# Cross-attention's sums turned through DRAM instead of by TensorE, one hop every half turn, in a fused decoder layer

## The reference, cut to what matters

```python
x = layernorm(x + self_attention(x))          # 16 heads of 16, causal over 64 rows
x = layernorm(x + cross_attention(x, c))      # channels = the 64 rows, time = the 256 columns
x = layernorm(x + feed_forward(x))            # 256 -> 1024 -> 256, quantised activations and weights

# cross_attention, b = 32, 8 heads of 8 channels, 256 positions each
q = rotary(split_heads(Wq @ x + bq)); k = rotary(split_heads(Wk @ c + bk)); v = split_heads(Wv @ c + bv)
p = softmax(einsum('bhtc,bhsc->bhts', q, k) / sqrt(8))
out = einsum('bhts,bhsc->bhtc', p, v)         # 256 x 8 per head
y = Wo @ out.transpose(0, 1, 3, 2).reshape(b, 64, 256) + bo
```

## Time and profile before

| | |
|---|---|
| median of 3 runs | 563.03 us (562.54 to 566.03) |
| the profiled execution | 563.8 us, of which its span is 561.9 us |
| PE busy | 450.6 us, 80% of the span |
| DVE busy | 442.4 us, 79% |
| ACT busy | 382.0 us, 68% |
| POOL busy | 289.6 us, 52% |
| granted TensorE clock, mean | 0.848 |
| DMA | 37.07 MB; the SP queue's packets took 22.8% of 16 engines' span |

### The profile page before, as it was taken

How to read it: one execution, slowest core, us unless ns; L and a number is a source line. 1 busy time by engine, 2 the same in 40 slices (tenths; PEclk the granted TensorE clock), 3 DMA queues, 4 the chain that set the end, 5 groups by cost and what they waited for, 6 DMA issues and landing times. The chain is left out here.

```text
span 561.9 us, 12026 instructions
## 1 busy us (share of the span) xinstructions
PE 450.6 (80%) x4162; PEld 243.0 (43%) x4162; DVE 442.4 (79%) x965; ACT 382.0 (68%) x698; POOL 289.6 (52%) x387
## 2 busy tenths in 40 slices
PE   6568799999999999999999999889877701555563
PEld 5354545555545555555555555433333200333342
DVE  2656687888988979889889798865848959999973
ACT  2222266767767667676676686687767787999972
POOL 5742565447555574475555744620032727667652
PEclk9677799999999999999999999975987875555555
DMA  6134318233242242332422323210000000000010
GB/s 217 48 97 149 97 46 248 66 92 91 57 111 67 64 110 60 90 91 60 108 69 64 106 61 82 71 56 1 3 1 1 1 0 1 10 28 19 30 37 29
DMA packets 51674, 37.07 MB, mean 66 GB/s; under 512 B 21408, under 2 KB 47648, under 8 KB 51488
## 3 DMA queue, kind: packets, MB, share of 16 engines
q1 hardware_dynamic: 51328, 36.10, 22.8%
q10 hardware_dynamic: 288, 0.23, 0.2%
HBM read 24.52 MB, written 10.49 MB: 62 GB/s over the span
## 5 line engine op out<-in xcount | busy, mean ns | idle before, releaser
L970 DVE TENSOR_REDUCE MX<-mx_b 128x2 f32<-128x512 f32 x256 | 167.8, 679 | 37.6 <-PE mx_b L581 36.4
L775 ACT ACTIVATE PB<-e_b 128x512 f32<-128x512 f32 x256 | 149.6, 592 | 64.7 <-PE e_b L609 63.8
L581 PE MATMUL mx_b<-KA,QA 48*128 48x256 bf16 x512 | 100.8, 282 | 10.3 <-DVE MX L970 10.1
L609 PE MATMUL e_b<-QA,KA 50*128 50x256 bf16 x512 | 100.9, 281 | 2.7 <-ACT PB L775 2.1
L626 PE MATMUL u_b<-PB,VA 128*32 128x256 f32 x1024 | 86.2, 404 | 3.4 <-ACT PB L775 2.9
L897 POOL TENSOR_TENSOR SP<-SP,srec 128x1024 f32<-128x1024 f32 x15 | 28.5, 1901 | 79.0 <-DVE srec L942 79.0
L581 PEld LDWEIGHTS mx_b<-KA,QA 48*128 48x128 bf16 x512 | 30.1, 95 | 88.5 <-issue 48.9
L1238 POOL TENSOR_TENSOR H<-H,row_tab 128x1024 f32<-128x1024 f32 x16 | 37.8, 2359 | 22.9 <-ACT H L1196 19.5
L1285 PE MATMUL r_b<-identh,Q 128*128 128x128 f16 x128 | 16.6, 311 | 39.5 <-ACT Q L1206 39.5
L1291 PE MATMUL z_b<-w2q,Q2T 128*128 128x256 bf16 x128 | 30.2, 417 | 19.3 <-ACT Q2T L1217 19.3
L314 POOL TENSOR_TENSOR rs<-mv,epsc 128x1 f32<-128x1 f32 x32 | 6.1, 189 | 72.5 <-DVE mv L301 50.2
(11 more groups left out here) (169 smaller groups left out, 1048.4 us busy)
## 6 DMA issues: line engine op xcount, KB each, us to landing
KA<-parts_k SPq DMA_DIRECT2D x64, 96.0 KB
QA<-parts_q SPq DMA_DIRECT2D x64, 96.0 KB
parts_q<-part_q SPq DMA_DIRECT2D x32, 128.0 KB, 2.0
parts_k<-part_k SPq DMA_DIRECT2D x16, 192.0 KB, 2.1
C<-in_ctx SPq DMA_DIRECT2D x16, 128.0 KB, 3.0
X<-in_x SPq DMA_DIRECT2D x16, 128.0 KB, 2.9
out_y<-O SPq DMA_DIRECT2D x16, 128.0 KB, 1.7
XT<-in_xT SPq DMA_DIRECT2D x15, 128.0 KB, 2.2
```

What stands on the lines that cost most here:

```text
L581: m = nc.tensor.matmul(mx_b[n % 2][:, D * k:D * k + D], QA[low:low + K_MAX, 2 * i.ring + b, h, P * u:P * u + P], KA[low:low + K_MAX, 2 * i ...
L609: m = nc.tensor.matmul(e_b[n % 2][:, D * k:D * k + D], KA[low:low + K_EXP, 2 * i.ring + b, h, P * sc:P * sc + P], QA[low:low + K_EXP, 2 * ...
L775: nc.scalar.activation(PB[:, n % 4].rearrange("p e t -> p (e t)"), e_b[n % 2][:, :], ACT.Exp, scale=XC ** -0.5).then_inc(e_sb.sem, 1)
L970: nc.vector.tensor_reduce(MX[:, b, e, 2 * q:2 * q + 2, u], mx_b[n % 2][:, :].rearrange("p (e s) -> p e s", e=2), AXL.X, ALU.max).then_inc( ...
```

## The change

The transposes that turn the sums, and the copy and the multiplications between them, are taken out. Instead:

- ACT writes `US` to a DRAM buffer (`store_sums`, two transfers of 256 KB per pair, at step 1 and step 9), right after its own copies.
- SP reads it back turned (`load_sums`): the denominators as `S32` (128 x 32, 16 KB) and the sums as `UV` (128 x 256, 128 KB), in the middle of the next turn.
- DVE takes one reciprocal of 128 x 32 (`reciprocals`, step 13). SP writes these 16 KB out (`recip_out`) and reads them back repeated over the channels (`recip_in`, 128 KB, into `RB`).
- POOL multiplies `UV` by `RB` into `AT` (`means`), one turn later than the means were made before. `x_out_proj` and all that follows for a pair are thus one turn later (`late` = pair `i-2` instead of `prev`).
- In the last turn two pairs pass through these steps: pair 13 (`late`) and pair 14 (`prev`), and the factors of pairs 0 to 13 are made at its end. Pair 15 passes through them in the second block, at later turns than before.
- The values' bias is folded into the output's once, in turn 0 (`value_bias`). The channel order of Wo is permuted on the host.
- In SP's turn the fan-out of the keys moves from the end of a turn to a place behind `max_rows(i, 1)` of the next, ahead of `load_c`.
- The identity table for the mask's product is written by two copies instead of one addition.

```diff
-        RD = sb("RD", [P, 16])
-        AN = sb("AN", [P, 2, 2, SEQ])
+        UV, RB = sb("UV", [P, D]), sb("RB", [P, D])
+        S32 = sb("S32", [P, 32])
...
+        def store_sums(sp, i, b):
+            if has(i, 2):
+                sp.wait_ge(ld_uv, 16 * (i.v - 1))
+                sp.wait_ge(ld_us, 16 * (i.v - 1))
+            wait(sp, u_sb, i, b + 1)
+            sp.dma_start(u_hbm[i.p][:, :, b].rearrange("c j x -> j c x"), US[:].rearrange("p s t -> p (s t)")).then_inc(moved[b], 16)
+
+        def load_sums(sp, i):
+            if has(i, 1):
+                wait(sp, at_sb, i.plus(-1), 1)
+            for b in range(2):
+                sp.wait_ge(moved[b], 16 * (i.v + 1))
+            flat = u_hbm[i.p].rearrange("c j b x -> c (j b x)")
+            sp.dma_start(S32[:], flat[XC:XC + 1].rearrange("c (r t) -> (c r) t", t=32)).then_inc(ld_us, 16)
+            sp.dma_start(UV[:], flat[0:XC].rearrange("c (r t) -> (c r) t", t=D)).then_inc(ld_uv, 16)
+
+        def recip_out(sp, i):
+            wait(sp, u_rec, i, 1)
...
+            sp.dma_start(rec_hbm.rearrange("h (k t) -> (h k) t", t=32), S32[:]).then_inc(rec_out, 16)
+
+        def recip_in(sp, i):
+            sp.wait_ge(rec_out, 16 * (i.v + 1))
+            sp.dma_start(RB[:], rec_hbm.unsqueeze(0).broadcast_to([XC, 16, D])).then_inc(rec_in, 16)
+
+        def reciprocals(dve, i):
+            dve.wait_ge(ld_us, 16 * (i.v + 1))
+            nc.vector.reciprocal(S32[:], S32[:]).then_inc(u_rec.sem, 1)
+
+        def means(pool, i):
+            pool.wait_ge(ld_uv, 16 * (i.v + 1))
+            pool.wait_ge(rec_in, 16 * (i.v + 1))
...
+            nc.gpsimd.tensor_tensor(AT[:], UV[:], RB[:], ALU.mult).then_inc(at_sb.sem, 1)
...
 # SP, body(i)
-                if i.v >= 1 and real(a):
-                    load_c(a)
                 if real(i):
                     max_rows(i, 1)
+                if i.v == NPAIR - 1:
+                    load_sums(sp, prev)
+                    recip_out(sp, prev)
+                    recip_in(sp, prev)
+                if i.v >= 0 and real(j):
+                    expand_rows("k", j)
+                if i.v >= 1 and real(a):
+                    load_c(a)
...
-                if real(a):
-                    expand_rows("k", a)
...
 # PE, body(i)
-                    if s == 3 and real(prev):
-                        u_transpose(pe, prev, 1, use(g_b[2], u_nrm, prev, 4))
-                    if s == 5 and real(prev):
-                        att_transpose(pe, prev, use(g_b[2], at_sb, prev, 1))
-                    if s == 9 and real(prev):
-                        x_out_proj(pe, prev, use(g_b[1], ln2, prev, 1))
+                    if s == 9 and real(late):
+                        x_out_proj(pe, late, use(g_b[1], ln2, late, 1))
+                    if s == 12 and i.v == NPAIR - 1:
+                        x_out_proj(pe, prev, use(g_b[2], ln2, prev, 1))
-                    if s == 13 and real(i):
-                        u_transpose(pe, i, 0, use(g_b[1], u_nrm, i, 2))
...
 # DVE, body(i)
-                    if s == 4 and i.v == NPAIR - 1:
+                    if s == 13 and i.v == NPAIR - 1:
                         mean_square(dve, 0)
-                    if s == 11 and i.v == NPAIR - 1:
-                        factors(dve, 0)
+                    if s == 15 and i.v == NPAIR - 1:
+                        factors(dve, 0)
+                        norm2_max(dve, prev)
...
 # POOL, body(i)
                 if i.v == NPAIR - 1:
+                    means(pool, late)
+                if real(late):
+                    rstd(pool, ln2, late, mv2, rs2)
+                if i.v == NPAIR - 1:
+                    means(pool, prev)
                     mean_power(pool, 0)
-                if real(prev):
                     rstd(pool, ln2, prev, mv2, rs2)
...
 # second block: pair 15, turns of the first product
+            load_sums(sp, last)
+            recip_out(sp, last)
+            recip_in(sp, last)
...
-                if t == 3:
+                if t == 6:
                     x_out_proj(pe, last, g_b[1])
...
-                if t == 1:
-                    u_norm(dve, last, 1, 1)
+                if t == 2:
+                    reciprocals(dve, last)
```

More of the change, by code:

```diff
@@ L238, in tile_at @@
             return i.plus(n // 16), n % 16
[L241 to L255, removed]
         def x_out_proj(pe, i, ps):
@@ L259, in x_out_proj @@
             nc.tensor.matmul(ps[:, 0:D], xw["o"], AT[:, :], start=True, stop=True).then_inc(xo_ps.sem, 1)
[L261 to L266, removed]
         def square_sum(act, i):
@@ new lines, in recip_in @@
+        def recip_in(sp, i):
[7 more added lines that the diff above has]
+            pool.wait_ge(rec_in, 16 * (i.v + 1))
+            if has(i, 1):
+                wait(pool, xo_ps, i.plus(-1), 1)
+            nc.gpsimd.tensor_tensor(AT[:], UV[:], RB[:], ALU.mult).then_inc(at_sb.sem, 1)
@@ L449, in body @@
                     store_parts("q", j)
+                if real(prev) and real(nxt):
+                    load_sums(sp, prev)
                 if real(nxt):
@@ L629, in pv_quad, with value_bias @@
                 last.then_inc(pv.sem, 1)
+            def value_bias(g):
+                ps = use(g_b[g], Event(s_bias, 0), Pair(0, 0), 1)
+                pe.wait_ge(ld_cross, NCROSS)
+                nc.tensor.matmul(ps[:, 0:1], xw["o"], xb["v"], start=True, stop=True).then_inc(s_bias_ps, 1)
             def weight_total(g):
@@ L859, in body @@
                         u_copy(i, 0)
+                    if s == 9 and real(i):
+                        store_sums(act, i, 0)
                     if s == 9 and real(nxt):
@@ L863, in body @@
                         pt_copy(a)
-                    if s == 13 and real(prev):
-                        norm2(act, prev)
+                    if s == (13 if real(nxt) else 12) and real(late):
+                        norm2(act, late)
+                    if s == (15 if real(nxt) else 12) and real(late):
+                        square_sum(act, late)
                     if s == 13 and real(a):
@@ L879, in _ @@
             u_copy(Pair(0, NPAIR - 1), 1)
+            store_sums(act, Pair(0, NPAIR - 1), 1)
         def k_mask(eng, ops, a, c, ev):
@@ L1116, in body @@
                     split_parts(pool, nc.gpsimd, "q", j)
+                if real(late) and real(nxt):
+                    means(pool, late)
                 if real(a):
@@ L1251, in _ @@
             mean_power(pool, 1)
+            means(pool, last)
             rstd(pool, ln2, last, mv2, rs2)
-            mean_power(pool, 2)
             for n in range(NPAIR):
+                if n == 5:
+                    mean_power(pool, 2)
                 wait(pool, qb, Pair(0, n), 1)
```

111 lines of the change are left out of this document (58 added, 53 removed).

## The result

The changed kernel takes **578.9 us** (median of 4 runs, 575.1 to 582.7) beside 564.5 for the kernel before on the same chip: ratio 1.025, 95% interval 1.017 to 1.034. Forecast were 556.8 and a range of 550 to 566. The profiled execution took 577.14, with a span of 575.0 against 561.9 and a granted clock of 0.819 against 0.848. Ratios, here and in the experiments, leave out executions more than 1.5% above the fastest of the same kernel.

A forecast was written before the change was run, and what follows sets the result against it. PE and DVE were taken to bound a turn by stretches, PE from step 13 to the next step 4. Terms -9.4 - 2.0 + 6.1 - 1.0 = -6.3 us against the profiled 563.8 gave 556.8 against the median, range 550 to 566.

The forecast's parts named there:

- Step 13: First block's turn: four transposes leave PE, one reciprocal replaces DVE's reciprocal and product; 0.57 us saved per turn.
- step 3: First block's turn: transposes go, but ACT's store issue of 0.43 us delays `MR`; 0.15 us saved, ends nothing and 0.59.
- lower end of 0.15 per turn: Smallest saving given for a steady turn of the first block, -2.0 us over 13 turns.
- first rival: Steady turns: both groups of transposes paid in full, 1.15 us per turn, total 551 us; chance 0.20.
- The Trainium skill's 50 ns: ACT's store issue: a dispatch of about 50 ns would hardly hold ACT and step 3 would pay 0.55 us; not followed.
- The turns together: First block before its last turn: -9.4 us for 13 steady turns and -2.0 for turns 13 and 14.
- turns 13 and 14: Late first block: same two groups of transposes, without scores behind the rotary; 1.0 us each, -2.0, ends 0 and -2.4.
- The keys' fan-out: SP's turn: moved ahead of `C`, which is issued about 210.6 and lands at 213.6, with 0.35 us to spare.
- third rival: Steady turns: `C` lands 4.9 us after issue instead of 3.0, PE stands 1.55 us per turn; 577 us, chance 0.10.
- The last turn: End of first block: pair 14's hops in series and POOL's power in the open cost +6.1 us, ends +3.5 and +9.
- +8.1 for slow writes to DRAM: Last turn's cost if the chain's two stores take the loads' 3.0 us, forecast 2.0 us later; not followed.
- The second block: Its start: transposes and DVE's 0.54 us go, DVE's reciprocal waits for store and load; -1.0 us, ends -2.6 and +2.

The follow-up runs named there:

- e1_rows9: The changed kernel with each store of the sums issued as four transfers of the 9 rows that are read, all in one step: 571.3 us, ratio 1.012 to the kernel before.
- e8_spread9: The changed kernel with each store as four transfers of 9 rows, one in each of four steps: 559.1 us, ratio 0.993 to the kernel before.

## Why the prediction was wrong

*Step 13 and step 3* (0.57 + 0.15 forecast): too low. (The lower end of 0.15 per turn fits neither: with nothing at step 3 the terms leave 0.57.) The undisturbed turn is 21.34 us, 1.15 below 22.49, which is the first rival's figure. The failed reading is that of the earlier trace rows: an issue of 0.43 on ACT's queue was taken for 0.43 of ACT. The row tells how long the queue is busy; the engine's earlier work runs beside it. The Trainium skill's 50 ns (DMA: Bandwidth & Descriptors, Anatomy of one DMA, for GpSimd's path), which was weighed there, is not what the row shows either (0.53 us), but its consequence, that ACT is hardly held, was the right one; the four-issue kernels show where it ends.

*The turns together* (-11.4 with turns 13 and 14): with the store spread they give -12.5 (301.3 us for 313.8), so the saving was well judged. In the changed kernel it is -0.1.

*The keys' fan-out* ("it fits with 0.35 us to spare", 0.10 for the third rival) is **the step that failed**, and with it the 2.3 us at which the sum took the store to land. `C` was issued when forecast (210.45 for 210.6 in the turn of the rows), but lands in 4.2 us (the median; 4.8 in that turn), not 3.0. The store takes 5.7 to 6.0 us and also holds the query rows back in three turns, for which the sum has no term. Of the 19.4 us by which the profiled span misses the forecast, 11.3 lie in the turns, 4.6 in the last turn and 3.9 behind it, less 0.5 ahead of them. The rival gave the point from which it decides as 3.8 us. The sum took the store as free: 256 KB from a pattern with four rows in front, in the window between the fan-out and `C`. What in the text spoke for the danger, the store issued by ACT in that window, was named and given too little. Its size was 577 by the rival's sum, and the time came out at 578.9. That this is so near is partly luck: the turns lose 12.4 and not 20, by two routes, and the end loses more. With its own rule and a landing of 4.2 the rival's sum gives only about +5.

*The last turn* (+6.1): +10.7. (The +6.1 runs to the issue of the last store; to the copy's end, as measured, it is +5.7.) The steps of the chain, forecast and in the changed kernel: store landed 2.3 and 6.0, denominators 2.3 and 1.7, out 2.0 and 1.4, in 2.8 and 6.2. The two small hops were over-priced by 1.2 in all, the store under-priced by 3.7 and `RB`, which pair 15's store held back, by 3.4; POOL's root took 2.60 in the open, not 3.55. Together that is +5.0, the whole of the miss. The runs bear it out: at like clock (0.61 and 0.62) the last turn is 24.8 us in the changed kernel and 20.8 in `e1_rows9`, whose last turn differs in the store alone. With the store spread (`e8_spread9`) `RB` lands in 2.9 us (397.38 to 400.33), but the turn is still +8.0, at half clock. What was left out there is pair 13's projection in step 9 at half clock: POOL's factor for pair 13 waited for it, and so did pair 14's means, until 403.57. The Trainium skill's rule on the write's receipt, from the same section (+8.1 for slow writes to DRAM), is not borne out in size: 1.40 us for the small write in this chain and 1.8 to 2.0 for the big ones with 32 or 128 in front, where the prediction put 3.0 by it. Whether a write is dearer than a load stays open: here it is 1.40 beside 1.69, but over the span the medians are 2.6 for the small write and 2.0 for the small load.

*The second block* (-1.0): +2.9, with a store of 5.7 us ahead of DVE's reciprocal:

```profile
435.25 0.35 DVE L291 RECIPROCAL S<-S 128x32 f32<-128x32 f32 x1 [5.43 <-DMA S<-u_hbm]
```

With the store spread it is -0.5.

So the plan of the sum holds for the kernel with the store repaired: -12.5 + 8.0 - 0.5, and 0.6 less ahead of the turns, -5.6 us of span against the forecast's -6.3, measured 559.1 us. Its terms are off by -1.1, +1.9 and +0.5, so that the total fits so well is partly luck. One term was missing: what the store's own pattern does to its landing and to the transfers beside it.

## What to carry to other kernels

Price a transfer from its pattern, not from its bytes: look at the first dimension on both sides, and take a landing time only from a row whose first dimension is as large. A transfer that is late can be late for two reasons together, as `C` was, so a remedy that works does not show that the other cause was none. Issues on a computing engine were free here as long as they were shorter than the work dispatched just ahead of them; spread them a step apart. When a row of the chain ends where an engine's own previous instruction ended, look for the transfer's real completion before you call the hop short.

## What the runs showed of the hardware

- The same 256 KB to DRAM: up to 107 GB/s (111 when alone), 4 completions and 5.7 to 6.0 us with 4 in front; up to 416 GB/s, 16 completions and 2.0 us with 128 in front; 1.8 us as four transfers with 32 in front.
- 4 KB beside such a store took 6.0 to 6.7 us to land. A load of 128 KB in eight parts took 6.2 us beside one: four of the parts came 2 us behind the other four.
- ACT's issues: one of 0.53 us leaves the turn at 21.34 us, as in the kernel with the store spread; 1.36 us of four in a row keeps the next activation back by 0.7 and a turn by 0.9 to 1.2 us. Four issues of 32 rows take 1.74 us, of 9 rows 1.36.
- 8.4 MB of well-spread stores more left the kernel before unchanged (0.997, 0.993 to 1.001).
